# A copy, a projection and an identity product moved between engines in the last stage of a graph network kernel

## The reference

```python
R = S + eye(N)
R = R / R.sum(-1, keepdims=True)
for n in range(2):
    A = top_p_attention(Xa, W1, W2, W3)   # softmax of q @ k.T, only the top 0.9 kept, rows sum to 1
    Xf = R @ Xf
    Xa = A @ Xa
    Z = Z + Xf @ U1[n].T + Xa @ U2[n].T
h = X + Z
out = (h - h.mean(-1)) / sqrt(h.var(-1) + 1e-5) * ln_g + ln_b
```

## Time and profile before

| | |
|---|---|
| median of three runs | 4404.75 us |
| the profiled execution | 4407.04 us, span 4405.2 us |
| PE busy | 3792.1 us, 86% |
| DVE busy | 3624.1 us, 82% |
| ACT busy | 3116.2 us, 71% |
| POOL busy | 1004.4 us, 23% |
| R products, L717 | 4096 instructions, 908.7 us |
| AV products, L813 | 4096 instructions, 902.2 us |
| unit-matrix products, L706 | 128 instructions, 39.0 us |

### The profile page before, as it was taken

How to read it: one execution, slowest core, us unless ns; L and a number is a source line. 1 busy time by engine, 2 the same in 40 slices (tenths; PEclk the granted TensorE clock), 3 DMA queues, 4 the chain that set the end, 5 groups by cost and what they waited for, 6 DMA issues and landing times.

```text
span 4405.2 us, 66289 instructions
## 1 busy us (share of the span) xinstructions
PE 3792.1 (86%) x25364; PEld 3171.0 (72%) x25364; DVE 3624.1 (82%) x6399; ACT 3116.2 (71%) x3129; POOL 1004.4 (23%) x1412
## 2 busy tenths in 40 slices
PE   8677777777777769999999679999999999999987
PEld 5677777777777747777777467777777777777776
DVE  2999999999999838888886498777778878898885
ACT  3789898889888845555554477777777777777761
POOL 0000000000000000001011243333333345555664
PEclk8899999999999979999999789999999999999998
DMA  3211111111111020000000212222322332333322
GB/s 116 90 46 63 46 63 46 63 44 65 44 66 44 28 69 14 19 16 19 16 19 17 81 50 90 85 91 91 91 86 82 119 94 88 104 106 106 100 89 86
DMA packets 131760, 292.49 MB, mean 66 GB/s; under 512 B 14123, under 2 KB 94187, under 8 KB 127059
## 3 DMA queue, kind: packets, MB, share of 16 engines
q1 hardware_dynamic: 131410, 287.99, 20.2%
HBM read 250.19 MB, written 37.75 MB: 65 GB/s over the span
## 4 chain that ended last, share of the span: by engine, by line
PE 63%; ACT 15%; issue 10%; POOL 4%; DVE 3%; DMA 2%; SPq 1%; ACTq 0%; POOLq 0%; DVEq 0%
PE ps L717 18%; PE ps L813 18%; PE ps L652 9%; ACT b L884 6%; PE ps L758 5%; PE ps L802 4%; ACT b L878 3%; ACT b L984 3%; PE ps L633 2%; ACT b L872 1%; PE ps L790 1%; PE ps L780 1%; DMA b<-in_adjTb 1%; SPq L293 1%; POOL b L479 1%
## 5 line engine op out<-in xcount | busy, mean ns | idle before, releaser
L717 PE MATMUL ps<-b 128*128 128x257 f32 x4096 | 908.7, 381 | 15.7 <-DMA b<-in_adjTb 15.6
L813 PE MATMUL ps<-b 128*128 128x257 f32 x4096 | 902.2, 380 | 0.0
L652 PE MATMUL ps<-cb,b 128*128 128x128 f32 x4096 | 607.9, 312 | 321.8 <-ACT b L878 321.8
L717 PEld LDWEIGHTS ps<-b 128*128 128x128 f32 x4096 | 777.5, 190 | 138.8 <-DMA b<-in_adjTb 19.5
L813 PEld LDWEIGHTS ps<-b 128*128 128x128 f32 x4096 | 771.6, 190 | 111.6
L652 PEld LDWEIGHTS ps<-cb,b 128*128 128x128 f32 x4096 | 547.3, 163 | 371.2 <-ACT b L878 329.5
L1164 DVE SCALAR_TENSOR_TENSOR b<-b 128x4096 f32<-128x4096 f32 x128 | 566.4, 4425 | 62.2 <-ACT b L872 58.8
L1166 DVE CUSTOM_DVE_ANT_0 b<-b 128x4096 f32<-128x4096 f32 x128 | 566.4, 4425 | 5.6 <-DMA b<-in_adj 1.3
L884 ACT ACTIVATE b<-ps 128x1024 f32<-128x1024 f32 x512 | 500.1, 1022 | 75.1 <-PE ps L652 73.7
L633 PE MATMUL ps<-b 128*64 128x128 f32 x8192 | 503.7, 276 | 0.0
L878 ACT ACTIVATE b<-b 128x4096 f32<-128x4096 f32 x128 | 474.3, 3706 | 8.1 <-DVE b L1168 8.1
(11 more groups left out here) (185 smaller groups left out, 4729.1 us busy)
## 6 DMA issues: line engine op xcount, KB each, us to landing
b<-in_adjTb SPq DMA_DIRECT2D x256, 512.0 KB, 3.9
b<-in_adj SPq DMA_DIRECT2D x32, 2048.0 KB, 8.0
y_d<-b SPq DMA_DIRECT2D x64, 128.0 KB, 1.7
h_d<-b SPq DMA_DIRECT2D x64, 128.0 KB, 1.8
b<-h_d SPq DMA_DIRECT2D x64, 128.0 KB, 2.2
b<-in_xT SPq DMA_DIRECT2D x1, 4096.0 KB, 15.0
b<-in_x SPq DMA_DIRECT2D x32, 128.0 KB, 2.2
b<-y_d SPq DMA_DIRECT2D x32, 128.0 KB, 2.0
```

Of the source, the lines that this page charges most:

```text
L652: last = nc.tensor.transpose(bank(2 * (gq % 3), 2)[:, b * 128:(b + 1) * 128], ub[:, u % UB, j * 128:(j + 1) * 128], ident_s)
L717: last = mm(b[:, 0:XA], aj[:, q % AJR, e, :], xf[:, j, :], start=False, stop=(j == NT - 1))
L813: last = mm(o[:, 0:XA], at[:, q % ATR, b, :], xa[:, j, :], start=(j == 0), stop=(j == NT - 1))
```

## The change

GpSimd adds the tile's rows of `xf` to the R product (257 columns, the one of ones too), and TensorE's opening product goes. On ScalarE, `av_ev` and `mq_ev` stand behind the second level in place of the first, the first R tile is copied behind the third level, and the second one behind the exponentials. On GpSimd, `final_add` stands ahead of `bracket`. There are three score buffers before and after.

```diff
@@ r_post
                         po.wait_ge(g["rd"], r + 1)
+                        plink(tt(prs[:, i, :], prs[:, i, :], xf[:, r % NT, :], ALU.add))
                         plink(tt(pq[:, 1, i:i + 1], prs[:, i, 256:257], mone, ALU.pow))
@@ the rounds of GpSimd
                         if n < NT:
                             levels(n)
+                        if n in fslot:
+                            final_add(fslot[n])
                         if n + 2 < NT:
                             bracket(n + 2)
-                        if n in fslot:
-                            final_add(fslot[n])
@@ Rstart and Rpart
                 def Rstart(r):
-                    b = rslot()
-                    if r >= NT:
-                        pe.wait_ge(s_xl[r % NT // CT], 48)
-                    mm(b[:, 0:XA], ident_s, xf[:, r % NT, :], start=True, stop=False)
-                    return b
+                    return rslot()
...
-                        last = mm(b[:, 0:XA], aj[:, q % AJR, e, :], xf[:, j, :], start=False, stop=(j == NT - 1))
+                        last = mm(b[:, 0:XA], aj[:, q % AJR, e, :], xf[:, j, :], start=(j == 0), stop=(j == NT - 1))
@@ acts
-                        if k == 1:
+                        if k == 2:
                             if 1 <= n <= NT:
                                 av_ev(n - 1)
                             if n >= 2 or n + 3 < NT:
                                 mq_ev(n - 2 if n >= 2 else None, n + 3 if n + 3 < NT else None)
-                        if k >= ACT_LEVELS - 1 and items:
-                            r_ev(items.pop(0))
-                    for r in items:
+                    for r in items[:1]:
                         r_ev(r)
                     if n + 2 < NT:
                         expo(n + 2)
+                    for r in items[1:]:
+                        r_ev(r)
```

## The result

The changed kernel takes 4335.57 us, the median of four runs (4333.98 to 4337.61); the kernel before took 4404.77 beside it (4403.72 to 4407.32). The ratio is 0.9842, with a 95% interval of 0.9825 to 0.9859: 69.2 us less, where 34.8 less was forecast (4370). The time lies within the range, and the sign and both halves of the mechanism came out; the gain is twice the forecast one, because one term of the early rounds was sized wrongly.

The account below looks back on a forecast made before the run. TensorE was to set early rounds at 52.6 us, a three-engine loop late ones at 63.1; -68.6, -7.8 and +41.9 gave -34.5 on the profiled execution, 4372.5, so 4370 us as median; range 4315 to 4425.

Parts of the forecast that it names:

- X(3): Moment the maximum over the partitions (L469) is out in round 3; forecast at 2701.0 us by the loop through three engines.
- 12 early rounds to X(15): L469's end in round 3 to round 15: first round 51.7 by TensorE, then 11 x 52.6 us.
- rounds 16 and 17: Rounds where R's second step waits for reloaded input: 2 x 52.6 plus twice the earlier excess, 6.3, giving 111.5 us.
- round 18: First late round, with half a final norm: 60.5 us forecast.
- 12 late rounds to X(30): Late rounds up to L469's end in round 30: 63.1 us each, set by the loop through GpSimd, ScalarE and VectorE.
- X(30) to the end: Tail after L469's end in round 30, taken as unchanged from the kernel before.
- 5.74 (scores to the next AV product): Last term of TensorE's early round, from the earlier trace, in 43.92 - 0.87 + 3.72 + 5.74 = 52.5 us.
- path (a): Late rounds: L542's second half goes first, L476 loses pass 2, L479 pass 3; L484 ends 23.2 us after L469's end.
- No wait: Early rounds: level 1's first copy on ScalarE was to start without waiting for L484's value.
- rival 2: Early rounds: L484 misses its gap before L1258 by 0.04 us, loop 54.5 us, +23 us: 4393; chance 10%.
- one more lost pass (4): Late rounds: GpSimd loses one more VectorE pass each, round 68.2 us, +61 us: 4431; chance 18%.
- Rival 3: Late rounds not held by lost passes: 58 us a round (4309), or 54 by VectorE alone (4260); chance 20%.

Follow-up runs that it names:

- part 1 undone: Changed kernel with the unit-matrix product on TensorE again and no 257-column addition on GpSimd: 4341.40 us, ratio 0.9852.
- undoing part 3: Changed kernel with the AV copy and the projection behind the first level again: 4265.88 us, ratio 0.9681.
- without the two: Changed kernel with the AV copy behind level 1 and the final addition behind the bracket again: 4292.68 us, ratio 0.9736.
- part 2 alone: Kernel before with only the R copies moved, first behind the third level, second behind the exponentials: 4282.00 us, ratio 0.9718.
- the best kernel: Changed kernel with the AV copy behind level 2 only up to round 16, then level 1, and SyncE's h store and load earlier: 4232.10 us, ratio 0.9604.

## Why the prediction was right in kind and short in size

By its own steps, in us of the profiled execution (4372.5 forecast, 4337.12 measured; the sum of the last column is the difference but for 0.1):

| step | forecast | measured | share of the miss |
|---|---|---|---|
| X(3) | 2701.0 | 2700.28 | -0.7 |
| 12 early rounds to X(15) | 630.3 | 610.0 (12 x 50.84) | -20.3 |
| rounds 16 and 17 | 111.5 | 108.55 | -3.0 |
| round 18 | 60.5 | 58.93 | -1.6 |
| 12 late rounds to X(30) | 12 x 63.1 | 12 x 62.38 | -8.6 |
| X(30) to the end | 110.1 | 109.0 | -1.1 |

**Part 2, the step that failed.** The forecast took the gap and the slow transposes out of TensorE's round, and kept "5.74 (scores to the next AV product)" as it stood in the earlier trace rows. That stretch was slow for the same reason as the transposes, and measures 4.12 after (2968.10 to 2972.22): 1.6 us too much in each early round, 12 times, and twice more in rounds 16 and 17, where the excess over two rounds was 6.9 for the forecast 6.3. The windows show it, first before, then after. Columns: stretch, its length, busy time of PE, PEld, DVE, ACT and POOL (with counts), granted clock of TensorE, DMA share, GB/s. The first group's second and third rows are the last transposes and the scores, the second group's rows transposes and scores:

```profile
2955.67:2958.45 2.78, 2.78 (x25) 2.54 (x23) 2.67 (x5) 2.39 (x2) 0.00 (x0) 1.00 0.53 149
2962.45:2964.35 1.90, 1.90 (x9) 1.57 (x9) 1.90 (x1) 1.78 (x2) 1.90 (x1) 0.50 0.00 0
2964.35:2969.66 5.31, 5.31 (x18) 2.17 (x18) 5.20 (x5) 3.71 (x4) 5.20 (x4) 0.69 0.00 0
```
```profile
2964.51:2968.10 3.59, 3.59 (x34) 3.42 (x32) 3.52 (x3) 2.84 (x4) 3.44 (x3) 1.00 0.46 146
2968.10:2971.73 3.63, 3.63 (x17) 1.46 (x17) 3.52 (x5) 3.63 (x5) 3.52 (x4) 1.00 0.01 5
```

After the gap the array ran at 0.50, that is at 1.2 GHz, through the transposes, and at a mean of 0.69 through the scores; without the gap both run at 1.00, that is at 2.4 GHz. The clock explains the whole of it: 3.63 us over 0.69 is 5.3. The Trainium skill, "TensorE: Matmul & The Clock Gate", section "Part 1: The HAM clock gate (the "warmup" mystery)", says that an idle array is held at half its clock and that activity gives the full one back; the rows agree. The forecast had looked at the durations of the transposes alone, and not at the granted clock of what follows them.

**Parts 3 and 4, the late rounds.** The mechanism was right link by link: L543's first addition held (its pair 4.02 us, from X+7.9), L476 and L479 held, L482 not, L484 at X+23.23 (23.2 forecast for path (a)), level 1 waiting up to 8.2 us for it (7), VectorE 8.4 for L469 (9). The Trainium skill's rule on the shared port pair ("SBUF — State Buffer", "Who interferes with whom") says that the first to start wins; the trace agrees for 256-column additions, of which a pair takes 1.41 us with no pass beside it. The loop closes on the measured round: over the rounds 18 to 29, from X to L484's end 23.1 us (23.3 forecast), from there to the end of L1022's copy 19.6 (19.65, and 0.1 for signals), to L515's end 2.3 (2.45), to the next X 17.4 (17.6), together 62.4. So the miss of 0.72 us a round is made up of small terms. The section on the change says "one level, not two, between the AV copy and the first R copy"; there is one level there in both kernels, and it is up to the exponentials that one stands in place of two. A run without the contention itself was not made: with no second operand in SBUF the search would be another program.

**Level 1 in early rounds.** "No wait" was wrong: it waits 2 to 3 us for L484, because TensorE's round became as short as GpSimd's loop (forecast 50.4, L484 at X+21.6 to 22.0 for 22.0), and because ScalarE is ready for it at T+9.1 (2973.58) and not at T+10.8, which was read in the earlier trace rows behind the slow score products. The wait costs TensorE nothing, as its transposes show (50.77 us apart); with part 1 undone it is gone. For the same reason VectorE waits 1.3 to 2.2 us for L469 in early rounds and not the 4 forecast.

**Part 1** was worth what was said for early rounds (0.87 us by TensorE's own starts, 0.7 from X to X) and nothing in late ones, and the additions were free in this kernel; 64 x 0.44 = 28 us was the bound, 6 us is the value.

**The rivals.** Neither the missed gap (rival 2) nor one more lost pass (4) happened: in the late round shown L484 ended at X+23.23, 2.8 us before L1255 started at 3690.25, and in the early ones it ended at X+21.6 to 22.0 each time. Rival 3 asked for a held addition to be free, and it was not; what it priced (late rounds of 54 to 58) is what undoing part 3 gives. The forecast was right that the late rounds give back gain, and the runs say how much: parts 3 and 4, forecast together, make the late rounds 62.4 us, where they take 58.5 without the two and 57.3 with part 2 alone.

## What to carry to other kernels

When a gap in TensorE's work is to go, take off with it all that runs at a lowered clock behind it, up to where the granted clock is full again; here the 4 us gap cost 6.6 us. Once a loop through several engines is the bound, an instruction that is put later inside it costs time each round, whatever it relieves elsewhere, though not always its full length: part 3 put a level of 9.5 us into the loop and cost 6.1 us a late round, because without it another wait set the round, and 2.2 in the kernel before. Part 3 was right only where TensorE set the pace, and the best kernel uses it in those rounds alone; part 4 was right only once part 3 was out of the late rounds. Price each part of a change in each stage by itself; here one part alone (part 2) was worth nearly twice the whole.

## What the runs showed of the hardware

- The cost of TensorE's gap goes on behind it: 8 transposes 1.90 us for about 0.93, 16 score products 5.31 to 5.86 for 3.65 to 3.70. After the 8.89 us gap of a late round the 80 products that follow take 19.18 us, against 14.08 for 64 at the full clock (17.6 for 80), 1.6 us more; the granted clock is 0.50 in the first 2.1 us of them, 0.75 in the next 2 and 1.00 from there on. In a late round this is hidden. The longer gap costs less behind it than the gap of 4 us does (2.6); why is not shown.

```profile
3755.37 10.60 PE L714 MATMUL ps<-b 128*128 128x257 f32 x48
3774.86 19.18 PE L714 MATMUL ps<-b 128*128 128x257 f32 x80 [8.89 <-DMA b<-in_adjTb]
```

- The maximum over the partitions costs GpSimd far more than its 0.39 us. In the last stage 5.7 to 7.5 us stand before it in which GpSimd runs nothing else (up to 10.3 in round 16), and behind it, where work is ready, 6.6 to 9.1 us. In the run without adjacency transfers the pause before it is 5.7 to 6.3 in all rounds but round 16. The timelines call both pauses "issue", but the traces hold more: GpSimd's sequencer has a `MODIFY_POOL_CONFIG`, which the program does not write, 5.5 to 7.4 us before each L469 of the last stage (round 16 apart) and another 0.35 us behind its start, under the line of the next instruction (L543 or L476), in every run. So both pauses begin with a change of GpSimd's configuration. That the change is what takes the time is read from its place; no run tested it.

- When GpSimd's 256-column addition had started first, VectorE's pass became 0.44 us longer (4.92 for 4.48), in all 14 late rounds of the changed kernel.

- The worth of an edit changed its sign with another one: part 4 costs 13 us beside part 3 (4335.6 against 4322.5) and saves 24 to 27 without it (4265.9 against 4292.7, in different groups).
